# The opening of an expert stage in another order: the first chunk's queries, scores and search ahead of the layer norm of the later tokens

## The reference: what is computed

```python
x_norm = x * inv * norm_w
q = (x_norm @ wq).reshape(B, T, 8, 2, 32)
sim = einsum('bthpd,hkpd->pbthk', q, keys)        # 64 keys, two halves
s1, i1 = top_k(sim[0], 16); s2, i2 = top_k(sim[1], 16)
all_scores = s1[..., :, None] + s2[..., None, :]
final_scores, pk = top_k(all_scores, 16)          # one of 64 * 64 experts each
hidden = gelu(einsum('btd,bthkd->bthk', x_norm, expert_down[final_idx]))
out = einsum('bthk,bthkd->btd', hidden * relu(final_scores), expert_up[final_idx])
```

## Time and profile before

| | |
|---|---|
| median of 3 runs | 2302.0 us (2298.33 to 2302.27) |
| the profiled execution | 2305.21 us, span from the first to the last instruction 2303.4 us |
| mean granted TensorE clock | 0.892 of full speed |
| busy: TensorE, VectorE | 1885.7 us (82%), 1611.6 us (70%) |
| busy: ScalarE, GpSimd | 755.8 us (33%), 578.4 us (25%) |
| transferred | 110.22 MB, 48 GB/s on average |

### The profile page before, as it was taken

The page is one execution under the profiler, slowest core; times in us unless marked ns, Lnnn a source line. Parts: engine busy times, 40 slices in busy tenths (PEclk is TensorE's granted clock), DMA queues, the critical chain, the costliest instruction groups (busy, mean ns, idle before and its releaser), DMA issues. The chain is left out here.

```text
span 2303.4 us, 48217 instructions
## 1 busy us (share of the span) xinstructions
PE 1885.7 (82%) x17564; PEld 1537.3 (67%) x17564; DVE 1611.6 (70%) x6862; ACT 755.8 (33%) x1633; POOL 578.4 (25%) x792
## 2 busy tenths in 40 slices
PE   6496799997359989989898898898888799728995
PEld 3364688875247778878777777787778677625663
DVE  3433566653999999999999999999982677320112
ACT  1343255553332322323323323223231355322220
POOL 2002244431004304224034042141241310030111
PEclk8697899997669999899999899999999799858997
DMA  2232444422600000000000000000000333212434
GB/s 62 68 105 47 109 109 103 102 63 63 161 2 5 3 5 6 2 6 6 2 6 6 2 6 2 6 6 2 2 2 8 82 84 83 86 51 72 152 101 126
DMA packets 90419, 110.22 MB, mean 48 GB/s; under 512 B 27168, under 2 KB 79088, under 8 KB 89552
## 3 DMA queue, kind: packets, MB, share of 16 engines
q1 hardware_dynamic: 84672, 99.09, 16.4%
q0 software_dynamic: 3344, 6.53, 0.8%
q10 hardware_dynamic: 2176, 1.61, 0.2%
HBM read 69.84 MB, written 33.83 MB: 45 GB/s over the span
## 5 line engine op out<-in xcount | busy, mean ns | idle before, releaser
L1572 POOL TENSOR_TENSOR peer_g<-peer_g,peer_qt 128x512 f32<-128x512 f32 (+1 forms) x208 | 250.2, 1214 | 707.6 <-ACT peer_qt L1800 707.6
L1685 PE MATMUL peer_out_ps<-peer_g,peer_up 128*128 128x256 f32 (+1 forms) x1664 | 371.8, 385 | 0.0
L1643 PE MATMUL peer_x_ps<-peer_xc,peer_dt 128*128 128x256 f32 (+1 forms) x1664 | 354.0, 375 | 0.0
L1685 PEld LDWEIGHTS peer_out_ps<-peer_g,peer_up 128*128 128x128 f32 x1664 | 319.3, 199 | 44.4
L1643 PEld LDWEIGHTS peer_x_ps<-peer_xc,peer_dt 128*128 128x128 f32 x1664 | 309.1, 193 | 40.2
L1284 DVE TENSOR_REDUCE l_attn_mx<-l_attn_s_ps 98x4 f32<-98x392 f32 (+1 forms) x320 | 174.8, 559 | 142.7 <-PE l_attn_s_ps L1054 102.7
L1675 PE MATMUL peer_x_ps<-peer_oh_h,peer_oh_a 128*128 128x32 bf16 x3136 | 167.3, 180 | 82.0 <-DVE peer_oh_l L2042 81.8
L1675 PEld LDWEIGHTS peer_x_ps<-peer_oh_h,peer_oh_a 128*128 128x128 bf16 x3136 | 162.7, 98 | 99.3 <-issue 58.9
L2038 DVE TENSOR_TENSOR peer_oh_a<-peer_a_t,peer_iota_f 128x8192 bf16<-128x8192 bf16 x49 | 216.4, 4416 | 0.0
L1205 ACT ACTIVATE l_attn_pt<-l_attn_st_ps 98x392 f32<-98x392 f32 x320 | 148.0, 491 | 150.5 <-PE l_attn_st_ps L1067 149.7
L1800 ACT ACTIVATE peer_qt<-peer_x_ps 128x512 f32<-128x512 f32 (+1 forms) x208 | 119.1, 572 | 236.7 <-PE peer_x_ps L1643 211.7
(11 more groups left out here) (333 smaller groups left out, 3457.4 us busy)
## 6 DMA issues: line engine op xcount, KB each, us to landing
moe_w<-in_L_ffn_w_dram SPq DMA_DIRECT2D x16, 1024.0 KB, 7.9
l_attn_pieces_q_dram<-l_attn_pieces_q SPq DMA_DIRECT2D x16, 294.0 KB, 4.5
l_attn_pieces_k_dram<-l_attn_pieces_k SPq DMA_DIRECT2D x16, 294.0 KB, 3.1
l_attn_stq<-l_attn_pieces_q_dram SPq DMA_DIRECT2D x16, 294.0 KB
l_attn_stk<-l_attn_pieces_k_dram SPq DMA_DIRECT2D x16, 294.0 KB
peer_g<-n_L_ffn_expert_down_dram SPq DMA_DIRECT2D x8, 512.0 KB
peer_up<-in_L_ffn_expert_up_dram SPq DMA_DIRECT2D x2, 2048.0 KB, 17.6
moe_expert_in<-l_blank SPq DMA_DIRECT2D x16, 197.5 KB
```

The source lines that it names most:

```text
L1572: nc.gpsimd.tensor_tensor(pair, pair, act_out[jp % 2][:, :, 0:cols], ALU.mult).then_inc(g_done, 1)
L1643: mm = nc.tensor.matmul(x_ps[b][:, jj * CT:jj * CT + cols], dt[:, k, 2 * jp + jj, :], xc[p][:, k, 0:cols], start=(k == 0), stop=(k == KC - 1))
L1685: mm = nc.tensor.matmul(out_ps[:, m * CT:m * CT + cols], up[:, j, m * P:(m + 1) * P], g[:, j, 0:cols], start=(j == 0), stop=(j == J - 1))
```

## The change

The work is the same, and so are its instructions; only the order on TensorE, ScalarE and VectorE differs, and SyncE and GpSimd are not edited. TensorE makes the first two means ahead of the key transposes. VectorE centres pieces 0 and 1, sums and squares, copies the keys, scales pieces 0 and 1, and takes pieces 2 and 3 as far as their squares. The first chunk's queries, both tiles' scores and the copies of them come then. VectorE searches tile 0, does a part of the norm of pieces 2 to 7, searches tile 1, and finishes the norm before `make_codes`.

```diff
--- before.py
+++ after.py
@@ -1691,23 +1691,27 @@
                         if (m, j) == TURN_AT and next_rows:
                             turn(n + 1, next_rows)
 
+            for n in range(2):
+                mean(n)
             pe.wait_ge(w_in, 16 * 2)
             for m in range(4):
                 mm = nc.tensor.transpose(tr_ps[:, m * NK:(m + 1) * NK], keys_n[:, m * P:(m + 1) * P], ident[0:NK, 0:NK])
             mm.then_inc(w_turned, 1)
             for n in range(2):
+                variance(n)
+            for n in range(2, 4):
                 mean(n)
-            for n in range(NLN):
+            queries(0, 0, CT)
+            pe.wait_ge(keys_ready, 1)
+            for t in range(NTILE):
+                scores(0, t, TT)
+            for n in range(4, NLN, 2):
+                for m in (n - 2, n - 1):
+                    variance(m)
+                for m in (n, n + 1):
+                    mean(m)
+            for n in range(NLN - 2, NLN):
                 variance(n)
-                if n + 2 < NLN:
-                    mean(n + 2)
-                if n == 1:
-                    queries(0, 0, CT)
-                if n == 3:
-                    pe.wait_ge(keys_ready, 1)
-                    scores(0, 0, TT)
-                if n == 5:
-                    scores(0, 1, TT)
             pe.wait_ge(ln_ready, NLN)
             pe.wait_ge(centred, NLN)
             for s in range(J // JS):
@@ -1770,16 +1774,21 @@
                 ins.then_inc(sim_ready, 1)
 
             act.wait_ge(eps_set, 1)
-            for i in range(NLN // 2):
-                for p in range(2):
-                    square(2 * i + p)
-                for p in range(2):
-                    root(2 * i + p)
-                if i == 1:
-                    query_out(0, CT)
-                if i == 2:
-                    score_out(0, 0, TT)
-            score_out(0, 1, TT)
+            for n in range(2):
+                square(n)
+            for n in range(2):
+                root(n)
+            for n in range(2, 4):
+                square(n)
+            query_out(0, CT)
+            for t in range(NTILE):
+                score_out(0, t, TT)
+            for n in range(2, NLN, 2):
+                for m in (n, n + 1):
+                    root(m)
+                if n + 2 < NLN:
+                    for m in (n + 2, n + 3):
+                        square(m)
             act.preload_act_table(ACT.Gelu)
             act.wait_ge(normed, NLN)
             for i in range(16):
@@ -1873,24 +1882,25 @@
                 add_halves(n)
             for n in range(2):
                 centre(n)
-            for i in range(NLN // 2):
-                for n in (2 * i, 2 * i + 1):
-                    if n + 2 < NLN:
-                        add_halves(n + 2)
-                    add_squares(n)
-                if i == 0:
-                    dve.wait_ge(nw_loaded, 16)
-                for n in (2 * i, 2 * i + 1):
-                    if n + 2 < NLN:
-                        centre(n + 2)
-                    scale(n)
-                if i == 1:
-                    dve.wait_ge(w_turned, 1)
-                    dve.wait_ge(iota_done, TOP + 3)
-                    for q in range(4):
-                        rows = slice(32 * q, 32 * q + 32)
-                        ins = nc.vector.tensor_copy(keys_b[rows, :, q * NK:(q + 1) * NK], tr_ps[rows, 0:4 * NK].rearrange("p (m k) -> p m k", m=4))
-                    ins.then_inc(keys_ready, 1)
+            for n in range(2, 4):
+                add_halves(n)
+            for n in range(2):
+                add_squares(n)
+            dve.wait_ge(w_turned, 1)
+            dve.wait_ge(iota_done, TOP + 3)
+            for q in range(4):
+                rows = slice(32 * q, 32 * q + 32)
+                ins = nc.vector.tensor_copy(keys_b[rows, :, q * NK:(q + 1) * NK], tr_ps[rows, 0:4 * NK].rearrange("p (m k) -> p m k", m=4))
+            ins.then_inc(keys_ready, 1)
+            dve.wait_ge(nw_loaded, 16)
+            for n in range(2):
+                scale(n)
+            for n in range(2, 4):
+                centre(n)
+            for n in range(4, 6):
+                add_halves(n)
+            for n in range(2, 4):
+                add_squares(n)
             chain = Chain(dve, own)
 
             def top16(values, indices, sources):
@@ -2047,8 +2057,24 @@
                 xs = x[:, :, bass.ds(n * CT, cols)]
                 nc.vector.tensor_tensor(xs, xs, out_ps[:, 0:KC * CT].rearrange("p (k t) -> p k t", k=KC)[:, :, 0:cols], ALU.add).then_inc(x_done, 1)
 
-            for t in range(NTILE):
-                top_halves(0, t, TT)
+            top_halves(0, 0, TT)
+            for n in range(4, 6):
+                centre(n)
+            for n in range(2, 4):
+                scale(n)
+            for n in range(6, 8):
+                add_halves(n)
+            for n in range(4, 6):
+                add_squares(n)
+            top_halves(0, 1, TT)
+            for n in range(6, 8):
+                centre(n)
+            for n in range(4, 6):
+                scale(n)
+            for n in range(6, 8):
+                add_squares(n)
+            for n in range(6, 8):
+                scale(n)
             make_codes(0, tile_rows(CT))
 
             def chunk(n, p, now, then):
```

## The result

The changed kernel takes 2314.3 us (median of 5 runs, 2304.67 to 2317.14), the kernel before 2300.66 beside it: ratio 1.0052 with an interval of 1.0032 to 1.0071. Twelve more runs of the unedited change, on another chip, gave 1.0032 (1.0016 to 1.0048). By these ratios it is slower by 7 to 12 us; the forecast was 2311.9, +9.9. The ratios leave out two runs of the seventh experiment, 2324 and 2325 us long at a mean granted clock of 0.88, where its others show 0.889 to 0.897.

What follows compares the result with a forecast made beforehand. VectorE was taken to carry the loop, so later first one-hots shift the end equally. expert_up landing at 657.6 plus 3.7 gave 661.3 against 651.36, +9.9 us: 2315.1 on the profiled execution, 2311.9 on the median's scale, range 2305 to 2315.5.

Steps and rivals of the forecast that it cites:

- X: End of the norm's last scale on VectorE: predicted 616.0, ends 613.9 and 618.5, 23.4 us later than before.
- The mechanism: Norm's end to SyncE's loads to TensorE: expert_up lands at 657.6, holds turn_weights(0), and first one-hots start 9.9 us later.
- a reserve: Before turn_weights(0) in the old order: expert_up was loaded 3.6 us earlier than needed.
- The rival of faster loads: SyncE's chain from X to expert_up shorter; landing at X + 31.7 is neutral; 2302 to 2306 us, chance 0.07.
- the estimate of 13.7 us: expert_up's 4.19 MB load by the skill's bandwidth limit, instead of 22.3 us; shift would be about +1.3 us.
- The rival of a hidden wait: expert_up in before X + 27.2, so one-hots start 4.4 us earlier (6 at full clock): about 2297 us, chance 0.06.
- the rival that something else is late behind X: Late transposes or a slow TensorE each add 2 to 4 us: 2314 to 2316 us, chance 0.12.
- its two conditions: First transposes at half clock miss X + 4.4, or TensorE stays at half clock through queries and scores (X at 618.5).
- four halves of a scale: VectorE between the searches, and again after them: 2.16 us each time, at 0.54 per instruction.
- the queries: TensorE's opening: 5.5 us, the middle between full clock and half (3.72 and 7.4), from about 563.5 to 569.0.
- The chain behind X: SyncE's stores and loads from the norm's end to expert_up's landing: 41.6 us, nothing of it set by another engine.

Runs made afterwards that it cites:

- the seventh experiment: Changed kernel with the expert_up wait moved, pieces 6 and 7 centred before the second search, a pair's means ahead of variances; ratio 0.9969, median 2297.11 us.
- once more: The changed kernel unedited, run again on another chip; ratio 1.0032, median 2309.24 us of 12 runs.
- experiment 1: Changed kernel with TensorE's wait for expert_up moved to just ahead of the first chunk's experts_out; ratio 0.9974, median 2295.23 us.
- experiment 3: Kernel before, old order, with expert_up loaded once more ahead of the load that counts, so it lands late; ratio 1.0054, median 2313.99 us.
- experiment 4: Changed kernel with the end of the norm ahead of the second search, all waits as they are; ratio 0.9994, median 2301.31 us.
- experiment 2: Kernel before with TensorE's expert_up wait moved to just ahead of the first chunk's experts_out; ratio 1.0005, median 2302.52 us.
- experiment 8: Changed kernel with the expert_up wait moved, plus GpSimd's index_steps(0) held until the norm is done; ratio 0.9982, inconclusive.
- ninth: The seventh experiment's kernel with GpSimd's second-tile candidates and index_steps(0) held until the norm is done; ratio 0.9991, median 2294.42 us.

## Why the prediction was right

| step, stage time in us | predicted | after | once more |
|---|---|---|---|
| first search | 18.8 | 19.2 | 17.7 |
| X, last scale ends | 62.3 | 63.85 | 62.36 |
| from X to `turn_weights(0)` | 41.6 | 42.1 | 41.9 |
| from there to the one-hots | 3.7 | 3.6 | 3.6 |
| VectorE idle ahead of them | about 15 | 15.9 | 15.7 |
| first one-hots | 107.6 | 109.5 | 107.8 |

The mechanism was the one forecast, and each link of it was seen: the one-hots follow expert_up (experiments 1 and 3), expert_up follows X (experiment 4), and in the old order it has a reserve that the move of X uses up (experiment 2). The rival of faster loads falls: issue to landing is again 22.3 us at most. With it falls the estimate of 13.7 us from the Trainium skill, DMA: Bandwidth & Descriptors; what the section Anatomy of one DMA gives as the fixed part is for transfers issued by GpSimd, and these are SyncE's. The two halves of expert_up landed one after the other, 12.9 and 22.3 us after issues that lie 0.5 us apart. The rival of a hidden wait falls too, though experiment 1 shows that it was worth what it said once the wait is moved (93.4 against the 97.7 and 99.7 of the old opening, for a forecast of 4.4 to 6 us).

So does the rival that something else is late behind X, but not by the time: 2314.3 lies in its range of 2314 to 2316 as well as in that of the forecast. The trace of the changed kernel excludes its two conditions. TensorE had made the first transposes by 611.0, X + 3.8, and the load of expert_down's third part followed at X + 3.9; and the queries ran at full clock. The medians of the two sets, 2314.3 and 2309.24, lie 2.4 us above and 2.7 us below the forecast; that it falls so near their middle is in part luck.

Of the 1.6 us by which X was late, 1.1 are four halves of a scale. I gave them 2.16 us; those of pieces 4 and 5 took 3.33, beside GpSimd. Another 0.4 lie ahead of the first search, where errors of both signs nearly cancel. I gave the queries 5.5 us, for a TensorE at half clock in part; they took 3.75 (554.38 to 558.13) and 3.62 in the second profile. But they started at 11.1, not at 9.8, behind the variances and means of the pieces before, which ran at half clock (four matmuls in 2.98 and 2.82 us, where 1.48 is the time at full clock); and from their end to the search it took 4.4 us where I had left 3.5. The clock was up when the queries came:

```profile
551.76 2.82 PE L1601 MATMUL peer_x_ps<-peer_dt,net_mean_w 128*128 128x392 f32 x4
554.38 3.75 PE L1621 MATMUL peer_sim_ps<-peer_up,peer_wq 128*128 128x256 f32 x16
...
564.43 1.48 PE L1606 MATMUL peer_x_ps<-peer_dt,net_mean_w 128*128 128x392 f32 x4
```

In the second profile they started at 9.7, and the search came 1.1 us earlier than forecast.

The chain behind X was 0.5 us longer than the 41.6 that I gave. I counted the 22.3 us from the issue of expert_up's first half, and they belong to the second, issued 0.5 us later. So the reserve of the old order was 3.1 us rather than 3.6.

The base had a scatter that I had not seen, with one profile in hand: the old opening gave one-hots at 97.7 and 99.7. Against these the shifts are 8.1 to 11.9, with 9.9 in the middle.

## What to carry to other kernels

Finding what a moved piece of work releases is worth more than summing what it saves. Here VectorE's chain became some 3 to 6 us shorter (`make_codes` at 63.8 and 62.3, against 66.7 and 68.8) and the kernel some 10 us slower, because the end of the norm, 21 to 25 us later, opens the buffers for a 42 us chain of loads with 3 us to spare. Put a wait just ahead of the first instruction that reads the data, not where the stage's setup ends; and before reordering a stage, try the single move that removes the first idle stretch: two means ahead of four transposes gave 5 to 8 us, and no reordering here is shown to give more.

## What the runs showed of the hardware

**VectorE and GpSimd slow each other, by the operation.** In the changed kernel the scales of 4 and 5 took 3.33 us beside GpSimd's `index_steps(0)`, and GpSimd's own subtraction was slower too:

```profile
598.47 0.88 POOL L1564 TENSOR_TENSOR peer_oh_a<-peer_oh_a 128x240 bf16<-128x240 f32 x1
...
599.80 1.04 POOL L1564 TENSOR_TENSOR peer_oh_a<-peer_oh_a 128x240 bf16<-128x240 f32 x1
```

With the two apart (experiment 8) it was 2.23 us on VectorE and, on GpSimd beside VectorE's search,

```profile
612.48 0.69 POOL L1564 TENSOR_TENSOR peer_oh_a<-peer_oh_a 128x240 bf16<-128x240 f32 x1
```

But the `centre` operations beside GpSimd's candidates kept their 0.97 us, and the candidates their 1.52. The same candidates beside `add_squares` and the scales, in the seventh experiment, took 2.84. First the changed kernel, then the seventh experiment:

```profile
596.32 1.52 POOL L1555 TENSOR_TENSOR peer_sc<-peer_v 128x128 f32<-128x128 f32 x4 [18.20 <-DVE peer_pad L1970]
...
608.85 2.84 POOL L1555 TENSOR_TENSOR peer_sc<-peer_v 128x128 f32<-128x128 f32 x4 [20.83 <-DVE peer_pad L1971]
```

`centre` reads one operand from PSUM; the scales read both tensors from SBUF. The Trainium skill, GPSIMD Engine Reference, section Specifications, says that GpSimd shares its SBUF interfaces with VectorE, with contention for VectorE instructions that have two SBUF inputs. These traces agree with it: 0.97 us kept for `centre`, 3.33 instead of 2.23 for the scales. No run changes the place of an operand alone, so the cause itself is not shown.

**TensorE's clock at the opening differs between executions of the same instructions.** In the profile of before the granted clock had risen by the first variance (0.95 from 562 to 564, stage time 8.3 to 10.3): it took 0.93 us, and the three means and variances behind it 0.82 each. In that of the second experiment, with the same opening, the clock stood at 0.50 until 561, stage time 16.5; the same four took 1.68 us and then 1.51 each, and the first search came 2 us later. The work ahead was the same; what decides between the two the runs don't show.

**It can also fall at the end.** In the profiled execution of experiment 4, which was its longest (2325 us), the granted clock fell at the start of the last chunk (0.63 from 1740 to 1742, 0.50 behind) and stayed down, although TensorE was busy without a break from 1740 to 1780. It had paused for 1.24 us just before; but so it had in the profile of before, for 1.25 us at the same place, where the clock stayed at 1.00. Windows of 20 us, columns as in the earlier trace rows:

```profile
1720.00:1740.00 20.00, 18.76 (x126) 15.73 (x125) 14.30 (x16) 1.36 (x5) 0.00 (x0) 1.00 0.00 0
1740.00:1760.00 20.00, 20.00 (x175) 20.00 (x171) 0.00 (x0) 5.11 (x14) 4.16 (x10) 0.51 0.01 2
1760.00:1780.00 20.00, 20.00 (x95) 20.00 (x95) 0.00 (x0) 1.66 (x6) 3.08 (x7) 0.50 0.00 1
```

At 1.00 (1720 to 1740) it is the engine's 2.4 GHz, at 0.50 its 1.2. The last addition on VectorE waited 57.7 us for TensorE there, against 31.5 in the profile of before, and those 26 us are about what this execution lies above its median. Single runs of the seventh and ninth experiments reached 2320 to 2325 us at a mean granted clock of 0.880 to 0.885, near this one's 0.880. That it was for the same reason is likely and not shown, since none of them was profiled.
